# A token mixer with a product-key expert layer: tie slots filled on GpSimd, weight quarters summed on TensorE, half of the kept gaps made on VectorE

## The chip, the core and the metric

The kernel runs on one core of a Trainium2 chip. The metric is the device time of one execution in microseconds (us); smaller is better. Three runs of the kernel before gave 279.06, 279.29 and 279.59 us, median 279.29.

## The reference, cut to what matters

The input x has 8 rows of 512 tokens with 128 features. After a layer norm it goes through an attention layer of three branches (blocks, selected tokens, windows) and, beside it, through a product-key layer of experts; the output is x + attention * silu(experts). The change touches only the expert layer:

```python
q = (x @ Wq.T).reshape(b, n, 2, HEADS, DIM_KEY).transpose(2, 0, 1, 3, 4)
sim = jnp.einsum('pbnhd,hkpd->pbnhk', q, keys)          # 2 halves x 8 heads, 32 keys each
sx, ix = jax.lax.top_k(sim[0], TOPK)                    # TOPK = 16
sy, iy = jax.lax.top_k(sim[1], TOPK)
all_scores = (sx[..., :, None] + sy[..., None, :]).reshape(b, n, HEADS, TOPK * TOPK)
scores, pk_indices = jax.lax.top_k(all_scores, TOPK)
h = jax.nn.gelu(jnp.einsum('bnd,bnhkd->bnhk', x, W_down[pk_indices]), approximate=False)
h = h * jax.nn.softmax(scores, axis=-1)
return jnp.einsum('bnhk,bnhkd->bnd', h, W_up[pk_indices])
```

So each token needs, for each of 16 key vectors (2 halves, 8 heads), the 16 largest of 32 scores, in order; and then for each head the 16 largest of the sums of pairs. Of the 256 pairs of ranks only 50 can be among the 16 largest; the kernel calls them candidates. The expert of a pair hangs on the ranks alone, so one column per candidate is enough, and its weight is summed over the heads.

## The kernel before

**Tiles and blocks.** The 4096 tokens are 32 tiles of 128 tokens (one per partition). Four tiles make a block, a row of the input (8 blocks, b = 0 to 7). A first part loads, normalises and transposes everything and handles the first tiles; then `turn(n)` runs for n = 4 to 31 on every engine, with n = 4b + j. In this text "turn j" is the turn with that j. There is no scheduler: each engine has a `turn` of its own with its calls in an order written by hand, and the engines meet at semaphores alone. Each engine works strictly in its own order, so a wait holds up all that is queued behind it.

**One tile on its way.** Tile n is handled over five turns. TensorE's `scores(n)` (L1541) writes 16 x 32 scores into one of two PSUM banks, two turns ahead. VectorE takes the largest 8 of each vector (`first_8`, L1138), marks the scores that are at least the eighth (`mark_above`, L1151), strikes them out in a copy `rest` (`strike_above`, L1159), and takes the next 8 (`next_8`, L1191). With equal scores more than 8 can be marked; for that `rest` has 8 more columns per vector, the tie slots. `sum_above` (L1168) counts the marks, `spill_above` (L1177) makes 2 * count - rank of it, and `put_ties` (L1185) fills each slot with the eighth score where the count reaches that far and with a very small number elsewhere. Counts and the value between stand in the PSUM bank of the scores, which is free for the next scores only after `put_ties` (`sim_used`). Then TensorE transposes the 16 ranks (`top_columns`), forms the 50 pair sums of each head (`pair_gaps`), ScalarE copies them out (`take_gaps`), VectorE finds a bound (`gaps_of_pairs`, `gaps_of_thirds`, `last_gaps`).

One turn later GpSimd subtracts the bound (`past_of`, L480), ScalarE takes the sign (`side_of`), TensorE transposes it (`transpose_sides`, L1570), ScalarE copies it out (`take_sides`), GpSimd squares it (`square_of`, L496), and TensorE counts for each candidate how many beat it (`count_places`, L1582), the last call of its turn for j = 0, 1 and 2. In the turn after, ScalarE turns the count into a large number for a candidate that is out (`out_by_of`, L731), GpSimd adds the gap (`drop_of`, L502), and ScalarE takes eight exponentials with sums (`exps`, L826). In the fourth turn VectorE inverts the sums (`invert_sums`), and GpSimd multiplies (`weigh`, L510), adds heads 0-3 to heads 4-7 (`add_halves`, L517) and the two halves of that (`add_quarters`, L524). TensorE transposes the result, two heads wide, into the expert weights (`expert_weights`, L1596).

**The order around the change.** GpSimd, turn 0: `past_of(n-2)`, `drop_of(n-3)`, `weigh`, `add_halves`, `add_quarters(n-4)`, `square_of(n-2)`, from b = 2 on `gelu_times_weights`, then `scale_probs`. Turn 1 the same to `square_of`. Turn 2: from b = 2 on `gate_silu`, then `past_of`, `weigh`, `drop_of`, `add_halves`, `add_quarters`, `square_of`, `norm2`. Turn 3: `past_of`, from b = 2 on `gate_attention`, `weigh`, `drop_of`, `add_halves`, `square_of`, `add_quarters`, and from b = 2 on `add_input`. VectorE, every turn: `strike_above(n)`, half of `first_8(n+1)`, `sum_above(n)`, in turn 0 the attention's `maxima`, `invert_sums(n-4)`, `spill_above(n)`, the other half of `first_8`, `put_ties(n)`, `mark_above(n+1)`, `next_8` in two halves with `gaps_of_pairs(n-1)` between, `gaps_of_thirds`, `last_gaps`. TensorE's turn 1 ends with `expert_weights(n-4)`, `scores(n+2)`, `count_places(n-2)`, and its turn 2 begins with `attention_out` (L1726), after which ScalarE does `row_squares` (L852), `take_gaps` and `take_sides`.

## Time and profile before

| | |
|---|---|
| median of three runs | 279.29 us |
| the profiled execution: its own time | 281.1 us |
| the profiled execution: span of the profile | 279.4 us |
| mean granted TensorE clock | 0.982 |
| busy share of the span: VectorE (DVE) | 93% |
| GpSimd (POOL), ScalarE (ACT), TensorE (PE) | 81%, 84%, 85% |

The profile is of one execution. Its span is the time from the first to the last instruction on the core; the execution's own time is 1.7 us longer. L12 is line 12 of the kernel, a start is in us from the start of the span, and "idle before" is how long the engine had nothing to run, with the instruction that ended it. On one engine an instruction can start before the one before it has ended, so what an instruction costs its engine is the distance between starts and not its duration. Every block from the third on looks like every other: the same instruction stands 28.16 us further on.

### The profile page before, as it was taken

Reading aid. Unit: us, or ns where it says so; the run is one execution under the profiler, and the core shown is the slowest. Engines: PE = TensorE matmul, PEld = TensorE weight load, DVE = VectorE, ACT = ScalarE, POOL = GpSimd, SP = SyncE. Lnnn points to the kernel's source line nnn. Section 1 sums busy time; section 2 is a strip of 40 time slices with the busy share of each in tenths; the row PEclk is TensorE's granted clock in tenths of the full one; section 3 lists DMA queues with packets and bytes.
Section 4 is the critical chain, followed back from the end, with each engine's and each line's share of the span. In section 5 each row is a group of like instructions: output and inputs, shape, how many; then the busy total and the mean of one; then the engine's idle time right before and its main releaser. Section 6 shows DMA issues by size and latency. Waiting matters only on the chain.

```text
span 279.4 us, 7039 instructions
## 1 busy us (share of the span) xinstructions
PE 237.8 (85%) x1562; PEld 176.8 (63%) x1562; DVE 259.9 (93%) x1715; ACT 235.6 (84%) x1048; POOL 226.0 (81%) x344
## 2 busy tenths in 40 slices
PE   7899689797889888978898889888988898879891
PEld 7456243575577667766776577657765776568690
DVE  5899999969999999999999999999999999995885
ACT  2554766868989999899999999999999999996853
POOL 7889701447688899989898989898989898989672
PEclk9999999979999999999999999999999999997997
DMA  7920000000000000010001000100010001000102
GB/s 179 279 74 1 2 0 0 2 1 0 5 0 0 5 0 1 13 31 0 2 3 40 1 0 5 39 0 5 0 39 4 1 0 41 1 1 4 38 1 77
DMA packets 11228, 6.23 MB, mean 22 GB/s; under 512 B 1457, under 2 KB 10674, under 8 KB 11186
## 3 DMA queue, kind: packets, MB, share of 16 engines
q1 hardware_dynamic: 9858, 5.12, 6.9%
q10 hardware_dynamic: 1328, 0.66, 1.1%
q8 instruction: 13, 0.21, 0.3%
q14 instruction: 29, 0.24, 0.3%
HBM read 3.67 MB, written 2.10 MB: 21 GB/s over the span
## 4 chain that ended last, share of the span: by engine, by line
PE 32%; ACT 32%; POOL 19%; issue 13%; DVE 3%; POOLq 0%; ACTq 0%; DVEq 0%
ACT prob L837 6%; PE scratch L1640 4%; PE sim L1548 4%; ACT p_win L936 3%; POOL past L485 3%; POOL squareT L500 3%; ACT gap L759 3%; PE t_bank L1566 3%; ACT away L971 3%; PE s_bank L1742 3%; PE s_bank L1736 2%; ACT spare L856 2%; PE s_bank L1531 2%; ACT sideT L747 2%; ACT side L729 2%
## 5 line engine op out<-in xcount | busy, mean ns | idle before, releaser
L1194 DVE MAX8 top<-rest 128x8 f32<-128x40 f32 x512 | 57.2, 184 | 0.1
L1144 DVE MAX8 top<-sim 128x8 f32<-128x32 f32 x496 | 54.0, 181 | 2.0 <-PE sim L1548 1.9
L837 ACT ACTIVATE prob<-drop 128x50 f32<-128x50 f32 x224 | 51.5, 255 | 0.0
L837 ACT ACTIVATION_READ_ACCUMULATOR prob<-drop 128x1 f32 x224 | 47.1, 212 | 0.0
L500 POOL TENSOR_TENSOR squareT<-sideT 100x512 bf16<-100x512 bf16 x31 | 32.3, 1041 | 6.7 <-ACT sideT L747 6.6
L513 POOL TENSOR_TENSOR wgt<-prob,rden 128x400 f32<-128x400 f32 x30 | 25.7, 855 | 11.8 <-DVE rden L1136 11.7
L1548 PE MATMUL sim<-sim_w,xT_all 128*128 128x512 f32 x64 | 34.7, 625 | 0.5 <-ACT xT_all L784 0.5
L485 POOL TENSOR_TENSOR past<-gap,last 128x400 f32<-128x400 f32 x31 | 26.8, 863 | 9.8 <-DVE last L1218 9.8
L507 POOL TENSOR_TENSOR drop<-gap,out_by 128x400 f32<-128x400 f32 x30 | 31.0, 1033 | 1.1 <-ACT out_by L736 1.1
L1566 PE MATMUL t_bank<-gaps_of,topT 128*128 128x200 f32 x128 | 29.2, 352 | 1.7 <-ACT topT L752 1.7
L1218 DVE MAX8 last<-slot_gap 128x8 f32<-128x22 f32 x256 | 24.4, 168 | 1.1
L1566 PEld LDWEIGHTS t_bank<-gaps_of,topT 128*128 128x128 f32 x128 | 20.7, 191 | 4.4 <-ACT topT L752 2.6
L1592 PE MATMUL f_bank<-count_s,sideT 101*128 101x100 bf16 x124 | 15.1, 208 | 9.8 <-POOL squareT L500 9.8
L1592 PEld LDWEIGHTS f_bank<-count_s,sideT 101*128 101x128 bf16 x124 | 11.5, 98 | 18.4 <-issue 18.4
L1171 DVE TENSOR_REDUCE sim<-above 128x16 f32<-128x512 bf16 x32 | 21.7, 678 | 0.1
L1156 DVE TENSOR_TENSOR above<-sim,top 128x512 bf16<-128x512 f32 x32 | 21.7, 677 | 0.0
L1164 DVE SCALAR_TENSOR_TENSOR rest<-above,sim 128x512 f32<-128x512 bf16 x32 | 21.4, 669 | 0.2
L747 ACT ACTIVATE sideT<-f_bank 100x512 bf16<-100x512 f32 x31 | 18.8, 607 | 1.3 <-PE f_bank L1578 1.2
L759 ACT ACTIVATE gap<-t_bank 128x400 f32<-128x400 f32 x32 | 16.2, 505 | 3.9 <-PE t_bank L1566 2.6
L729 ACT ACTIVATE side<-past 128x400 bf16<-128x400 f32 x32 | 17.2, 536 | 2.0 <-POOL past L485 2.0
L521 POOL TENSOR_TENSOR wgt<-wgt 128x200 f32<-128x200 f32 x29 | 17.7, 609 | 1.1
L1647 PE MATMUL scratch<-xT_all,wc_sb 128*128 128x128 f32 x64 | 16.2, 409 | 0.0
(295 smaller groups left out, 753.1 us busy)
## 6 DMA issues: line engine op xcount, KB each, us to landing
out<-y_sb SPq DMA_DIRECT2D x7, 256.0 KB, 2.3
x_sb<-in_L_attn_hidden_states SPq DMA_DIRECT2D x2, 256.0 KB, 4.0
fwq_sb<-in_L_ffn_Wq ACTq DMA_DIRECT2D x2, 256.0 KB, 5.8
x_sb<-in_L_attn_hidden_states SPq DMA_DIRECT2D x1, 512.0 KB, 5.4
wc_sb<-in_L_attn_Wc SPq DMA_DIRECT2D x1, 256.0 KB
out<-last_y SPq DMA_DIRECT2D x2, 128.0 KB, 1.9
wo_in<-in_L_attn_Wo SPq DMA_DIRECT2D x1, 192.0 KB
keys_sb<-in_L_ffn_keys ACTq DMA_DIRECT2D x1, 128.0 KB, 3.4
```

The costliest lines, as they stand in the source:

```text
L485: nc.gpsimd.tensor_tensor(past[:, :, :], gap[n % 4][:, :, :], last8[n % 2][:, :, 7:8].to_broadcast([P, HEADS, CANDS]), ALU.subtract).then_ ...
L500: nc.gpsimd.tensor_tensor(squareT[0:TWO, :], sideT[0:TWO, :], sideT[0:TWO, :], ALU.mult).then_inc(square_done, 1)
L507: nc.gpsimd.tensor_tensor(drop[:, :, :], gap[n % 4][:, :, :], out_by[:, :, :], ALU.add).then_inc(drop_done, 1)
L513: nc.gpsimd.tensor_tensor(w[:, :, :], prob[n % 2][:, :, :], rden[n % 2][:, :].unsqueeze(2).to_broadcast([P, HEADS, CANDS]), ALU.mult).then ...
L759: nc.scalar.activation(gap[n % 4][:, :, :].rearrange("p h c -> p (h c)"), t_bank[:, 0:HEADS * CANDS], ACT.Copy).then_inc(gap_out, 1)
L837: last = nc.scalar.activation(prob[d][:, h, :], drop[:, h, :], ACT.Exp, scale=-1.0, accum_out=den[d][:, h:h + 1])
L1144: last = nc.vector.max(top[n % 3][:, v, 0:8], sim_bank[n % 2][:, bass.ts(v, KEYS)])
L1194: last = nc.vector.max(top[n % 3][:, v, 8:16], rest[:, v, :])
L1218: last = nc.vector.max(last8[n % 2][:, h, :], slot_gap[:, h, :])
L1548: mm(sim_bank[n % 2][:, :], xT_all[:, bass.ts(n, P)], sim_w[:, :], start=True, stop=True).then_inc(sim_ready, 1)
L1566: last = mm(t_bank[:, bass.ts(k, HALF_H * CANDS)], topT[:, bass.ts(k, P)], gaps_of[:, :, :].rearrange("p h c -> p (h c)"), start=True, sto ...
L1592: mm(o, one[0:TWO + 1, bass.ts(k, P)], count_s[0:TWO + 1, :], start=True, stop=False)
```

## The change

It does three things, and an order goes with each.

1. For the tiles of the turns (n = 4 to 31) the tie slots are filled by GpSimd: `ties_of(n)`, three instructions of 128 x 128 elements, stands right behind `past_of(n-2)` in GpSimd's turn (in turn 2 `gate_silu` goes behind both). The counts and the value between stand in SBUF (`counts`, `tie`, `tie_off`), since GpSimd works on SBUF here. VectorE's turn begins with `sum_above(n)`, ahead of `strike_above(n)`, and has neither `spill_above` nor `put_ties`; `next_8` waits for GpSimd (`ties_done`). The bank of the scores is free after `strike_above`. One small constant, `tie_rank`, is made by GpSimd at the start. Tiles 0 to 3 keep VectorE's two instructions.
2. `add_quarters` is gone: TensorE's `expert_weights` adds the quarters with two accumulating products in place of one transpose, and `wgt4` has two buffers instead of one.
3. For 14 tiles (3, 4, 7, 8, ... 27, 28; in turns 2 and 3) `out_by_of` on ScalarE and `drop_of` on GpSimd are replaced by one VectorE instruction, `keep_gaps`, which reads the counts from PSUM and takes the larger of the two values.

```diff
 rest = sb("rest", [P, VECS, KEYS + 8])
+counts = sb("counts", [P, VECS])
+tie_off = sb("tie_off", [P, VECS, 8])
+tie = sb("tie", [P, VECS, 8])
+tie_rank = sb("tie_rank", [P, 8])
 topT = sb("topT", [P, 2 * P])
...
 def summed(n):
     return n >= TILES - 4
+def kept_by_vector(n):
+    return TB - 1 <= n < TILES - 3 and n % TB in (0, TB - 1)
+def out_bys_until(n):
+    return sum(not kept_by_vector(m) for m in range(n + 1))
 def sums_until(n):
...
                         allow_small_or_imprecise_dtypes=True))
+    nc.gpsimd.tensor_scalar(tie_rank[:, :], rank_row[:, 7:15], 0.5, None, ALU.mult)
     def place(n_done, ins):
...
     def drop_of(n):
-        pool.wait_ge(out_by_done, n + 1)
+        if kept_by_vector(n):
+            return
+        pool.wait_ge(out_by_done, out_bys_until(n))
         if n >= 1:
...
     def add_halves(n):
         pool.wait_ge(wgt_done, n + 1)
-        w = wgt[n % 2]
-        nc.gpsimd.tensor_tensor(wgt4[:, :, :], w[:, 0:HEADS // 2, :], w[:, HEADS // 2:HEADS, :],
-                                ALU.add).then_inc(wgt4_done, 1)
-    def add_quarters(n):
-        pool.wait_ge(wgt4_done, n + 1)
         if n >= 2:
             pool.wait_ge(c_ready, n - 1)
-        nc.gpsimd.tensor_tensor(wgt2[n % 2][:, :, :], wgt4[:, 0:2, :], wgt4[:, 2:4, :],
-                                ALU.add).then_inc(wgt2_done, 1)
+        w = wgt[n % 2]
+        nc.gpsimd.tensor_tensor(wgt4[n % 2][:, :, :], w[:, 0:HEADS // 2, :], w[:, HEADS // 2:HEADS, :],
+                                ALU.add).then_inc(wgt4_done, 1)
+    def ties_of(n):
+        pool.wait_ge(summed_above, n + 1)
+        pool.wait_ge(top_done, 2 * n)
+        nc.gpsimd.tensor_tensor(tie[:, :, :], counts[:, :].unsqueeze(2).to_broadcast([P, VECS, 8]),
+                                tie_rank[:, :].unsqueeze(1).to_broadcast([P, VECS, 8]),
+                                ALU.subtract).then_inc(tie_step, 1)
+        pool.wait_ge(tie_step, 2 * (n - TB) + 1)
+        nc.gpsimd.tensor_scalar(tie_off[:, :, :], tie[:, :, :], SPILL, 0.0, ALU.mult, ALU.min
+                                ).then_inc(tie_step, 1)
+        pool.wait_ge(tie_step, 2 * (n - TB) + 2)
+        nc.gpsimd.tensor_tensor(rest[:, :, KEYS:KEYS + 8], tie_off[:, :, :],
+                                top[n % 3][:, :, 7:8].to_broadcast([P, VECS, 8]),
+                                ALU.add).then_inc(ties_done, 1)
     def gelu_times_weights(b):
...
         b, j = divmod(n, TB)
         if j == 0:
             past_of(n - 2)
+            ties_of(n)
             drop_of(n - 3)
             weigh(n - 4)
             add_halves(n - 4)
-            add_quarters(n - 4)
             square_of(n - 2)
             if b >= 2:
                 gelu_times_weights(b - 2)
             scale_probs(b - 1)
         elif j == 1:
             past_of(n - 2)
+            ties_of(n)
             drop_of(n - 3)
             weigh(n - 4)
             add_halves(n - 4)
-            add_quarters(n - 4)
             square_of(n - 2)
         elif j == 2:
+            past_of(n - 2)
+            ties_of(n)
             if b >= 2:
                 gate_silu(b - 2)
-            past_of(n - 2)
             weigh(n - 4)
             drop_of(n - 3)
             add_halves(n - 4)
-            add_quarters(n - 4)
             square_of(n - 2)
             norm2(b - 1)
         else:
             past_of(n - 2)
+            ties_of(n)
             if b >= 2:
                 gate_attention(b - 2)
             weigh(n - 4)
             drop_of(n - 3)
             add_halves(n - 4)
             square_of(n - 2)
-            add_quarters(n - 4)
             if b >= 2 and n < TILES - 1:
                 add_input(b - 2)
...
     def out_by_of(n):
+        if kept_by_vector(n):
+            return
         act.wait_ge(count_ready, n + 1)
...
             dve.wait_ge(summed_above, n)
+            dve.wait_ge(sim_used, n)
         nc.vector.tensor_tensor(above[:, :, :], sim_bank[n % 2][:, :].rearrange("p (v k) -> p v k", k=KEYS),
...
                                        sim_bank[n % 2][:, :].rearrange("p (v k) -> p v k", k=KEYS),
-                                       ALU.mult, ALU.add).then_inc(struck, 1)
+                                       ALU.mult, ALU.add).then_inc(sim_used, 1)
     def sum_above(n):
-        dve.wait_ge(struck, n + 1)
-        nc.vector.tensor_reduce(sim_bank[n % 2][:, 0:TIES], above[:, :, :], AX_X, ALU.add
-                                ).then_inc(summed_above, 1)
-    def tie_slots(n):
-        return sim_bank[n % 2][:, TIES:TIES + 8 * VECS].rearrange("p (v k) -> p v k", v=VECS)
+        dve.wait_ge(above_done, n + 1)
+        if n >= 1:
+            dve.wait_ge(ties_done, n)
+        nc.vector.tensor_reduce(counts[:, :], above[:, :, :], AX_X, ALU.add).then_inc(summed_above, 1)
     def spill_above(n):
         dve.wait_ge(summed_above, n + 1)
-        nc.vector.scalar_tensor_tensor(tie_slots(n),
-                                       sim_bank[n % 2][:, 0:TIES].unsqueeze(2).to_broadcast([P, VECS, 8]), 2.0,
+        nc.vector.scalar_tensor_tensor(tie[:, :, :], counts[:, :].unsqueeze(2).to_broadcast([P, VECS, 8]), 2.0,
                                        rank_row[:, 7:15].unsqueeze(1).to_broadcast([P, VECS, 8]),
...
     def put_ties(n):
         dve.wait_ge(spill_done, n + 1)
-        nc.vector.scalar_tensor_tensor(rest[:, :, KEYS:KEYS + 8], tie_slots(n), SPILL, eighth(n, 8),
-                                       ALU.mult, ALU.min).then_inc(sim_used, 1)
+        if n >= 1:
+            dve.wait_ge(top_done, 2 * n)
+        nc.vector.scalar_tensor_tensor(rest[:, :, KEYS:KEYS + 8], tie[:, :, :], SPILL, eighth(n, 8),
+                                       ALU.mult, ALU.min).then_inc(ties_done, 1)
     def next_8(n, h):
         dve.wait_ge(sim_used, n + 1)
+        dve.wait_ge(ties_done, n + 1)
         for v in range(h * HALF_V, (h + 1) * HALF_V):
...
                                 negate=True).then_inc(max_done, 1)
+    def keep_gaps(n):
+        dve.wait_ge(count_ready, n + 1)
+        dve.wait_ge(gap_out, n + 1)
+        dve.wait_ge(prob_done, n)
+        nc.vector.scalar_tensor_tensor(drop[:, :, :].rearrange("p h c -> p (h c)"),
+                                       f_bank[:, 0:HEADS * CANDS], OUT_SCALE,
+                                       gap[n % 4][:, :, :].rearrange("p h c -> p (h c)"),
+                                       ALU.mult, ALU.max).then_inc(drop_done, 1)
     def first_turns():
...
     def turn(n):
         b, j = divmod(n, TB)
+        sum_above(n)
         strike_above(n)
...
             first_8(n + 1, [0])
-        sum_above(n)
         if j == 0:
...
         invert_sums(n - 4)
-        spill_above(n)
+        if kept_by_vector(n - 3):
+            keep_gaps(n - 3)
         if n + 1 in tiles:
             first_8(n + 1, [1])
-        put_ties(n)
-        if n + 1 in tiles:
             mark_above(n + 1)
...
             pe.wait_ge(slot_gap_done, 2 * TILES)
+        elif n >= 1 and kept_by_vector(n - 1):
+            pe.wait_ge(drop_done, n)
         elif n >= 1:
-            pe.wait_ge(out_by_done, n)
+            pe.wait_ge(out_by_done, out_bys_until(n - 1))
         for k in range(HEADS // 2):
...
         o = dst[0:TWO, bass.ts(n % TB, P)]
-        if n < TILES - TB:
-            pe.wait_ge(wgt2_done, n + 1)
-            last = nc.tensor.transpose(o, wgt2[n % 2][:, :, :].rearrange("p h c -> p (h c)"), ident[:, :])
+        if n <= TILES - TB:
+            pe.wait_ge(wgt4_done, n + 1)
+            w, heads = wgt4[n % 2], HEADS // 2
+        elif n < TILES - 1:
+            pe.wait_ge(wgt_done, n + 1)
+            w, heads = (wgt if n < TILES - LAST else last_wgts)[n % 2], HEADS
         else:
-            if n == TILES - TB:
-                pe.wait_ge(wgt4_done, n + 1)
-                w, heads = wgt4, HEADS // 2
-            elif n < TILES - 1:
-                pe.wait_ge(wgt_done, n + 1)
-                w, heads = (wgt if n < TILES - LAST else last_wgts)[n % 2], HEADS
-            else:
-                pe.wait_ge(last_wgt, 1)
-                w, heads = last_wgts[n % 2], HEADS
-            for h in range(0, heads, 2):
-                last = mm(o, w[:, h:h + 2, :].rearrange("p h c -> p (h c)"),
-                          ident[:, :], start=(h == 0), stop=(h == heads - 2))
+            pe.wait_ge(last_wgt, 1)
+            w, heads = last_wgts[n % 2], HEADS
+        for h in range(0, heads, 2):
+            last = mm(o, w[:, h:h + 2, :].rearrange("p h c -> p (h c)"),
+                      ident[:, :], start=(h == 0), stop=(h == heads - 2))
         last.then_inc(c_ready, 1)
```

## Rows read from the trace of the kernel before

**Rows 1.** Busy time of each engine in one block of four turns, 193.16 to 221.32.
```profile
193.16:221.32 28.16, 24.61 (x171) 18.95 (x171) 27.47 (x197) 27.16 (x132) 26.31 (x36) 1.00 0.04 11
```

The columns of rows 1 are the stretch and its length, the busy us of PE, PEld, DVE, ACT and POOL, each with its number of instructions, the granted clock, the DMA share and GB/s.

**Rows 2.** The chain that ended last: start, us, the window exponentials of three blocks.
```profile
64.75 1.24 ACT p_win L936 x8
...
92.50 1.24 ACT p_win L936 x8
...
233.37 1.24 ACT p_win L936 x8
```

**Rows 3.** GpSimd's instructions in order of time in that block: start, us, what [idle before].
```profile
192.72 1.04 POOL L500 TENSOR_TENSOR squareT<-sideT 100x512 bf16<-100x512 bf16 x1 [0.24 <-ACT sideT L747]
...
197.86 1.04 POOL L507 TENSOR_TENSOR drop<-gap,out_by 128x400 f32<-128x400 f32 x1
...
199.43 1.03 POOL L500 TENSOR_TENSOR squareT<-sideT 100x512 bf16<-100x512 bf16 x1
...
202.02 0.85 POOL L485 TENSOR_TENSOR past<-gap,last 128x400 f32<-128x400 f32 x1
...
204.35 0.86 POOL L513 TENSOR_TENSOR wgt<-prob,rden 128x400 f32<-128x400 f32 x1 [0.49 <-DVE rden L1136]
205.28 0.61 POOL L521 TENSOR_TENSOR wgt<-wgt 128x200 f32<-128x200 f32 x1
205.97 0.40 POOL L528 TENSOR_TENSOR wgt<-wgt 128x100 f32<-128x100 f32 x1
206.32 1.04 POOL L500 TENSOR_TENSOR squareT<-sideT 100x512 bf16<-100x512 bf16 x1
...
210.27 0.86 POOL L485 TENSOR_TENSOR past<-gap,last 128x400 f32<-128x400 f32 x1
...
214.05 1.04 POOL L500 TENSOR_TENSOR squareT<-sideT 100x512 bf16<-100x512 bf16 x1
...
220.88 1.04 POOL L500 TENSOR_TENSOR squareT<-sideT 100x512 bf16<-100x512 bf16 x1 [0.24 <-ACT sideT L747]
```

**Rows 4.** TensorE in order of time: first product of two of the counts.
```profile
200.61 0.20 PE L1592 MATMUL f_bank<-count_s,sideT 101*128 101x100 bf16 x1 [0.34 <-POOL squareT L500]
...
215.30 0.21 PE L1592 MATMUL f_bank<-count_s,sideT 101*128 101x100 bf16 x1
```

**Rows 5.** ScalarE in order of time: the last step before the square.
```profile
220.18 0.62 ACT L747 ACTIVATE sideT<-f_bank 100x512 bf16<-100x512 f32 x1
```

**Rows 6.** Groups of instructions on GpSimd, by shape: mean ns after the comma.
```profile
L463 POOL TENSOR_SCALAR xn_all<-x_sb,rstd,nmr 128x128 f32<-128x128 f32 x16 | 7.0, 453 | 0.4
...
L573 POOL TENSOR_TENSOR p_cs<-p_cs,rgate 128x128 f32<-128x128 f32 x7 | 2.8, 400 | 0.0
L575 POOL TENSOR_TENSOR p_cs<-p_cs,rgate 64x64 f32<-64x64 f32 x7 | 2.0, 287 | 0.0
...
L408 POOL TENSOR_SCALAR off_mean<-ident 128x128 f32<-128x128 f32 x1 | 0.6, 552 | 0.0
```

**Rows 7.** VectorE in order of time, turn 1 of that block.
```profile
210.96 0.30 DVE L1180 SCALAR_TENSOR_TENSOR sim<-sim,rank_row 128x128 f32<-128x128 f32 x1
211.17 0.88 DVE L1144 MAX8 top<-sim 128x8 f32<-128x32 f32 x8
211.96 0.27 DVE L1188 SCALAR_TENSOR_TENSOR rest<-sim,top 128x128 f32<-128x128 f32 x1
212.15 0.68 DVE L1156 TENSOR_TENSOR above<-sim,top 128x512 bf16<-128x512 f32 x1
212.75 0.90 DVE L1194 MAX8 top<-rest 128x8 f32<-128x40 f32 x8
```

**Rows 8.** VectorE near the end: the kept gaps of the last two tiles.
```profile
266.01 0.56 DVE L1420 SCALAR_TENSOR_TENSOR last_drop<-f_bank,gap 128x400 f32<-128x400 f32 x1
266.49 0.55 DVE L1420 SCALAR_TENSOR_TENSOR last_drop<-t_bank,gap 128x400 f32<-128x400 f32 x1
```

**Rows 9.** GpSimd at the start of the span.
```profile
6.36 0.23 POOL L452 TENSOR_SCALAR var<-mv 128x4 f32<-128x4 f32 x1
```

More of the change, by code:

```diff
@@ L235, in program @@
         wgt = [sb(f"wgt{i}", [P, HEADS, CANDS]) for i in range(2)]
-        wgt4 = sb("wgt4", [P, HEADS // 2, CANDS])
-        wgt2 = [sb(f"wgt2_{i}", [P, 2, CANDS]) for i in range(2)]
+        wgt4 = [sb(f"wgt4_{i}", [P, HEADS // 2, CANDS]) for i in range(2)]
         last_drop = [sb(f"last_drop{i}", [P, HEADS, CANDS]) for i in range(2)]
@@ L274, in program @@
         sim_ready, sim_top8, sim_used, top_done = sem("sim_ready"), sem("sim_top8"), sem("sim_used"), sem("top_done")
-        above_done, struck, summed_above, spill_done = (
-            sem(n) for n in ("above_done", "struck", "summed_above", "spill_done"))
+        above_done, summed_above, spill_done, tie_step, ties_done = (
+            sem(n) for n in ("above_done", "summed_above", "spill_done", "tie_step", "ties_done"))
         topT_ready, topT_out, gap_ready, gap_out = (sem(n) for n in ("topT_ready", "topT_out", "gap_ready", "gap_out"))
@@ L286, in program @@
         half_out = sem("half_out")
-        wgt_done, wgt4_done, wgt2_done, c_ready, c_out = (
-            sem(n) for n in ("wgt_done", "wgt4_done", "wgt2_done", "c_ready", "c_out"))
+        wgt_done, wgt4_done, c_ready, c_out = (
+            sem(n) for n in ("wgt_done", "wgt4_done", "c_ready", "c_out"))
         last_past, last_square, last_kept, last_wgt, blocks_scaled = (
```

## The prediction

> **What bounds the kernel now.** I read the busy time of a block first, then the chain that ended last, then each engine in order of time. In a block of 28.16 us VectorE is busy 27.47, ScalarE 27.16, GpSimd 26.31, TensorE 24.61 [rows 1]. Three engines are within 7% of full, so no share of busy time says which one sets the period; an engine that is 97% busy may still be waiting in step with a loop through the others. The chain says so: between the window exponentials at 92.50 and at 233.37 [rows 2] there are five blocks of 28.17 each, and the chain in them runs through GpSimd, TensorE and ScalarE, hardly through VectorE. The interval before, 64.75 to 92.50, is 27.75: there GpSimd lacks the work that starts with b = 2.
>
> The loop of one block has three legs. They all stand in GpSimd's order of time [rows 3]:
> - **Leg A**, from `past` in turn 0 (202.02) to `squareT` in turn 1 (214.05): 12.03, GpSimd alone, with one wait of 0.49 for VectorE's reciprocal (at 204.35).
> - **Leg B**, from there to `squareT` in turn 2 (220.88): 6.83. GpSimd's own work is not what fills it. The square ends at 215.09, and TensorE starts to count at 215.30 [rows 4]. `count_places` is the last call of its turn 1, and `attention_out` is queued behind it, then ScalarE's row squares and copies of gaps and sides, the last from 220.18 for 0.62 [rows 5], and then the next square.
> - **Leg C**, from `squareT` in turn 2 (192.72) to `past` in turn 0 (202.02): 9.30, GpSimd alone without a wait.
>
> Sum 12.03 + 6.83 + 9.30 = 28.16. In leg B the handoff from a square to TensorE takes 0.15 where TensorE waits for it (the square of turn 3 runs from 199.43 for 1.03 [rows 3], TensorE follows at 200.61 [rows 4]), and here 0.21 pass. So TensorE's own queue has only some 0.06 us to spare: nearly all that delays the square of turn 1 delays the whole block.
>
> **The change, part by part.**
>
> *Tie slots on VectorE, removed.* The distance between starts is what counts: 210.96 to 211.17 and 211.96 to 212.15 [rows 7], 0.21 + 0.19 = 0.40 us in each of 28 turns.
>
> *Kept gaps on VectorE, added.* The nearest instruction is the same form at the end: 266.01 to 266.49, 0.48 us [rows 8], in two turns of four. VectorE's block gets 4 x 0.40 - 2 x 0.48 = 0.64 us lighter, 26.83 of work. The new order (count before strike) moves no work. Counts written to SBUF and not to PSUM: I cost it at nothing; one element is written for 32 read.
>
> *Tie slots on GpSimd, added.* Three instructions of 128 elements per partition. The first and third read two tensors: 0.40 us by the row of that very size [rows 6]. The second reads one: 0.45 by the two-operation form (453 ns), 0.55 by the one-operation form (552 ns) [rows 6]; I take 0.45, since it has two operations. Each of the second and third needs the one before: where an instruction waits for its forerunner the handoff is 0.08 (205.28 + 0.61 to 205.97 [rows 3]), where it doesn't, starts overlap ends by 0.04. So a tie fill holds GpSimd for 0.40 + 0.07 + 0.45 + 0.07 + 0.40 - 0.04 = 1.35 us. Bounds: 1.0 if each costs no more than the 64-element row (0.29) with the handoffs, 1.6 if the rows of 8 elements cost more than those of 50 and 80 that I see.
>
> Of the one-input instruction the rows say 453 ns, more than the 400 of two inputs. The Trainium skill (GPSIMD Engine Reference, 4.1 Engine selection) says that GpSimd is about half as fast as VectorE on two inputs but roughly at line rate on one. By that page the second instruction would take an estimated 0.3 us, a tie fill 1.2, and the time would be 284.1; the rows of this trace speak against it.
>
> *Quarters, removed.* A quarter starts at 205.97 and the square behind it at 206.32: 0.35, and the handoff before it goes too (205.28 to 205.97 becomes 0.57), so 0.47 in turns 0, 1 and 2, and 0.35 in turn 3, where the square stands between. TensorE gets two products in place of one transpose, one instruction more per turn: at the mean of rows 1, 24.61 / 171, some 0.14 us. I cost it at nothing, since TensorE has 3.5 us free per block; in turn 1 it stands ahead of the count, and that waits for the square anyway once the square is late. Without that cover it would add its 0.14 to leg B.
>
> *`drop` on GpSimd, removed in turns 2 and 3.* It lasts 1.04 us (197.86 [rows 3]), of which the next start overlaps 0.04: 1.00, less 0.10 because `add_halves` now follows directly on the `weigh` it needs: 0.90. ScalarE loses two `out_by`; neither stands between TensorE's count and the square in leg B, so I count no gain.
>
> *The constant at the start.* `tie_rank` stands between the last iota and the first variance, whose input VectorE has had ready (GpSimd ran into it without a wait at 6.36, 0.23 us [rows 9]). The chain goes through there: +0.2 us, once.
>
> **The loop after the change.**
> - Leg A: 12.03 - 0.49 (the reciprocal, which is no later, is now hidden behind the tie fill) + 2 x 1.35 - 2 x 0.47 = 13.30. No `drop` of turns 0 and 1 is taken away: those two stay on GpSimd.
> - Leg B: square 1.04, handoff 0.15, and from TensorE's count (215.30) to the next square (220.88) 5.58 as before: 6.77. GpSimd's own work between the squares (+1.35 for the tie fill, -0.90, -0.47) stays near 5.9 and waits at the end for the copy of the sides.
> - Leg C: 9.30 + 1.35 - 0.90 - 0.35 = 9.40.
>
> Sum 29.47, which is 1.31 more than 28.16. GpSimd's relief lies in the wrong turns: the two `drop`s go from turns 2 and 3, and the one in turn 2 is within leg B, where GpSimd has slack, while both tie fills of leg A lie on the loop.
>
> The new wait on VectorE: in turn 1 the `past` of GpSimd moves from 210.27 [rows 3] by -0.49 + 1.35 - 0.47 to 210.66, its tie fill ends near 212.9; VectorE would come to `next_8` at 212.75 - 0.40 = 212.35 [rows 7]. It waits 0.5 us, and half of `next_8`, the gaps and `last_gaps` are queued behind; but `past` of turn 2 isn't due before 216, so it costs nothing here. VectorE has 29.47 - 26.83 = 2.6 us per block for such waits.
>
> Over the run: five intervals, +6.6. From 233.37 on there is one leg A and B more, +1.2, after which the end hangs on other work that the change leaves alone. The interval from 64.75 to 92.50 has GpSimd idle and VectorE nearly full: -0.5, of its 0.64. Start +0.2. Together +7.5: a span of 279.4 + 7.5 = 286.9 and 288.6 for the profiled execution against its own 281.1. The profiled span is within 0.1 of the median of the runs, so the median goes from 279.29 to **286.8**. With tie fills between 1.15 and 1.6 the loop moves by 3 x -0.20 to 3 x 0.25 per block, some six blocks: 283.2 to 291.3.
>
> **The rivals.**
>
> *GpSimd alone is the bound (12%).* If leg B shrinks, say because ScalarE, freed of an `out_by`, delivers the sides sooner, the loop can't be shorter than GpSimd's own work. Busy 26.31 [rows 1] - 4 x 0.36 - 2 x 1.00 + 4 x 1.25 = 27.9, with handoffs about 28.7, 0.5 above 28.16: 279.3 + 6 x 0.5 - 0.3 = 282. For it: ScalarE is 27.16 busy now and gets lighter. Against: from 215.30 to the square at 220.88 the chain that ended last goes through TensorE and ScalarE with no wait for anything else, and the `out_by` isn't in it.
>
> *VectorE was the bound and is relieved (10%).* It is the busiest engine, 27.47 of 28.16. If the small instructions of the tie fill are so cheap on GpSimd that one holds it for less than about 0.91 us (1.35 - 1.31/3), the loop is no longer than before, and lighter VectorE and ScalarE let the block shrink by up to 0.64: 279.3 - 6 x 0.6 = 275.7. That point, 0.91, is where the sign turns. Against it: it is below three times the 287 ns of the 64-element row with the handoffs, 1.0.
>
> *VectorE waits for the ties and falls behind (7%).* If GpSimd reaches the tie fill in turns 0 to 2 a further us late, `next_8` slips by as much, the next `last_gaps` is late for `past`, and GpSimd and VectorE take turns waiting. One us more in two of four turns, partly hidden: 292 or more.
>
> **How the numbers follow.** The forecast, the loop through the square of turn 1, has 68% and by itself 283.2 to 291.3; GpSimd alone 12%; relieved VectorE 10%; late ties 7%; everything cancels 3%. The range reaches down to the second case and up to the forecast's own upper end: 281.5 to 291. A measurement of this kernel can tell about 0.2% from no change (0.6 us). Faster 0.10, same 0.03, slower 0.87.
>
> **What the profile after would show.** Right: window exponentials 29.5 us apart; the three tie instructions at 0.40, 0.45 and 0.40; TensorE idle before its count in turn 1, in place of none; GpSimd waiting near 0.9 us for the copy of the sides before the square of turn 2; VectorE's busy share down to about 88%, with a wait for GpSimd before the first `next_8` in turn 1. Wrong: a tie fill under 1.0 us; blocks of 28.7 or less with GpSimd never idle; or `past` waiting on `last_gaps`, which would mean that VectorE sets the pace.

## The result and the profile after

The change makes the kernel slower: median 295.04 us (four runs, 293.39 to 296.21) against 279.44 us of the kernel before beside it (279.06 to 279.95), ratio 1.0536 with a 95% interval of 1.0499 to 1.0572. The direction was forecast, the size was not: +7.5 forecast, +15.6 measured, and 295.04 lies outside the range of 281.5 to 291.

The profiled execution after took 294.93 us, its span is 293.2. From profile to profile that is +13.8; the profiled execution of before was itself 1.7 above its median, and the one of after is not. All that follows is counted from profile to profile. Some executions of a kernel show a lower granted clock and take over 1.5% longer than its fastest; the ratios and medians of the experiments below are of the others.

The page of the kernel after, its first and fourth part and one of its groups:

```profile
span 293.2 us, 7306 instructions
PE 247.7 (84%) x1646; PEld 186.6 (64%) x1646; DVE 258.0 (88%) x1673; ACT 232.0 (79%) x1034; POOL 241.3 (82%) x387
POOL 49%; PE 24%; issue 13%; ACT 11%; DVE 2%; POOLq 0%; DVEq 0%; ACTq 0%
...
L548 POOL TENSOR_SCALAR tie_off<-tie 128x128 f32<-128x128 f32 x28 | 17.9, 639 | 2.4
```

VectorE went from 93% to 88% busy, as forecast, and is only 2% of the chain that ended last; GpSimd is half of it, where it was 19% before. One block, 199.97 to 230.45, in the columns of rows 1:

```profile
199.97:230.45 30.48, 26.14 (x185) 20.40 (x184) 27.24 (x192) 26.73 (x129) 28.45 (x42) 1.00 0.04 10
```

It is 30.48 us long instead of 28.16 [rows 1], and GpSimd is now the busiest engine. Its instructions in order of time, that block, against [rows 3]:

```profile
199.97 1.04 POOL L512 TENSOR_TENSOR squareT<-sideT 100x512 bf16<-100x512 bf16 x1 [0.86 <-ACT sideT L773]
...
209.65 0.87 POOL L497 TENSOR_TENSOR past<-gap,last 128x400 f32<-128x400 f32 x1
...
218.50 0.85 POOL L497 TENSOR_TENSOR past<-gap,last 128x400 f32<-128x400 f32 x1
219.32 0.40 POOL L544 TENSOR_TENSOR tie<-counts,tie_rank 128x128 f32<-128x128 f32 x1
219.81 0.64 POOL L548 TENSOR_SCALAR tie_off<-tie 128x128 f32<-128x128 f32 x1
220.53 0.42 POOL L551 TENSOR_TENSOR rest<-tie_off,top 128x128 f32<-128x128 f32 x1
220.91 1.03 POOL L521 TENSOR_TENSOR drop<-gap,out_by 128x400 f32<-128x400 f32 x1
...
222.83 0.61 POOL L537 TENSOR_TENSOR wgt<-wgt 128x200 f32<-128x200 f32 x1
223.40 1.03 POOL L512 TENSOR_TENSOR squareT<-sideT 100x512 bf16<-100x512 bf16 x1
...
230.45 1.04 POOL L512 TENSOR_TENSOR squareT<-sideT 100x512 bf16<-100x512 bf16 x1 [0.86 <-ACT sideT L773]
```

The legs read off these starts:

| leg | before | forecast | after |
|---|---|---|---|
| A, `past` turn 0 to `squareT` turn 1 | 12.03 | 13.30 | 13.75 |
| B, to `squareT` turn 2 | 6.83 | 6.77 | 7.05 |
| C, to `past` turn 0 | 9.30 | 9.40 | 9.68 |
| block | 28.16 | 29.47 | 30.48 |

TensorE in order of time, turn 1 of that block, against [rows 4]:

```profile
223.49 0.68 PE L1654 MATMUL c_bank<-ident,wgt 128*100 128x128 f32 x4 [0.90 <-POOL wgt L537]
224.01 1.02 PE L1584 MATMUL sim<-sim_w,xT_all 128*128 128x512 f32 x2
224.87 0.21 PE L1630 MATMUL f_bank<-count_s,sideT 101*128 101x100 bf16 x1
```

And the same stretch in the chain that ended last:

```profile
222.83 0.62 POOL wgt L537
223.45 0.04 issue
223.49 0.68 PE c_bank L1654 x4
224.17 0.86 PE sim L1584 x2
```

Here is something that the forecast did not have: the chain leaves GpSimd before the square. TensorE waits 0.90 for the halves, does the products (four passes for two fp32 products) and the scores, and only then counts, 1.47 after the square's start. The square alone would have let it count after 1.04 + 0.15.

The kernel before has to be read again here, in leg A, which the forecast took for GpSimd's alone. The chain that ended last leaves GpSimd there: from `past` in turn 0 it goes over ScalarE and then through TensorE's own queue into the count:

```profile
208.23 1.12 ACT prob L837 x9
...
214.60 0.86 PE sim L1548 x2
```

The count follows the scores at 215.30 without a wait, while the square would have allowed it at 215.09 + 0.15 = 215.24. So it is the square, with GpSimd's leg A before it, that had 0.06 to spare, and TensorE's queue had nothing. The two ways were almost equally long; the tie fills lengthened that of GpSimd, and it took over.

**Where the 13.8 us are**, by the first window exponential of a block in each trace: up to the first -1.47 (63.17 against 64.64; forecast +0.2); the next interval +0.72 (28.47 against 27.75; forecast -0.5); the five intervals after it +11.15 (152.03 against 140.88; forecast +6.6); from there to the end +3.4 (49.5 against 46.1; forecast +1.2).

Part of the ends is TensorE's clock. Before, it was granted 0.61 between 58 and 62, and 1.00 after. The chain runs through TensorE there in both; the scores, before and after:

```profile
59.20 1.71 PE sim L1548 x2
...
58.73 0.86 PE sim L1584 x2
```

That is 0.85, and the three projections around them took 0.75, 0.64 and 0.49 on the chain before and 0.39, 0.33 and 0.33 after: 1.68 together. Without the clock the start would have been 0.21 later, not 1.47 earlier, and the count ahead of these instructions does start 0.21 later (57.48 against 57.27). After, the clock falls near the end, and the products and scores of the last leg B take 1.18 and 1.71 on the chain, where the block above has 0.68 and 0.86: 1.35 of the end's loss. The window of the kernel after, in the columns of rows 1:

```profile
252.00:256.00 4.00, 3.08 (x10) 1.76 (x9) 3.53 (x25) 4.00 (x23) 3.92 (x6) 0.72 0.01 2
```

TensorE's instructions in it, in order of time:

```profile
253.96 1.18 PE L1654 MATMUL c_bank<-ident,wgt 128*100 128x128 f32 x4 [0.90 <-POOL wgt L537]
254.93 1.92 PE L1584 MATMUL sim<-sim_w,xT_all 128*128 128x512 f32 x2
```

### The profile page after: what moved, and what is told of

The parts are those of the page before. It is cut to its first block, busy times and chain, and to the rows that moved or that the text cites. A ratio compares the mean times of both kernels' runs of the same rounds, so it can differ in the third digit from the quotient of the medians.

```text
span 293.2 us, 7306 instructions
## 1 busy us (share of the span) xinstructions
PE 247.7 (84%) x1646; PEld 186.6 (64%) x1646; DVE 258.0 (88%) x1673; ACT 232.0 (79%) x1034; POOL 241.3 (82%) x387
## 4 chain that ended last, share of the span: by engine, by line
POOL 49%; PE 24%; issue 13%; ACT 11%; DVE 2%; POOLq 0%; DVEq 0%; ACTq 0%
POOL squareT L512 8%; POOL wgt L527 6%; POOL past L497 5%; POOL tie_off L548 4%; PE sim L1584 4%; POOL drop L521 3%; PE s_bank L1776 3%; POOL y L622 3%; POOL actT L560 3%; POOL tie L544 2%; PE s_bank L1770 2%; ACT spare L882 2%; PE s_bank L1567 2%; ACT sideT L773 2%; PE c_bank L1654 2%
## 5 line engine op out<-in xcount | busy, mean ns | idle before, releaser
L1654 PE MATMUL c_bank<-ident,wgt 128*100 128x128 f32 x112 | 18.5, 289 | 12.3 <-POOL wgt L537 12.3
L1654 PEld LDWEIGHTS c_bank<-ident,wgt 128*100 128x100 f32 x112 | 14.2, 170 | 19.5 <-issue 10.5
L778 ACT ACTIVATE topT<-t_bank 128x256 f32<-128x256 f32 x32 | 12.5, 390 | 12.7 <-PE t_bank L1593 12.7
L1200 DVE TENSOR_REDUCE counts<-above 128x16 f32<-128x512 bf16 x32 | 21.5, 670 | 0.0
L548 POOL TENSOR_SCALAR tie_off<-tie 128x128 f32<-128x128 f32 x28 | 17.9, 639 | 2.4
```

Of the source, the lines that this page charges most:

```text
L548: nc.gpsimd.tensor_scalar(tie_off[:, :, :], tie[:, :, :], SPILL, 0.0, ALU.mult, ALU.min).then_inc(tie_step, 1)
L1654: last = mm(o, w[:, h:h + 2, :].rearrange("p h c -> p (h c)"), ident[:, :], start=(h == 0), stop=(h == heads - 2))
```

## The experiments

Theory 1: the block is the loop through the square of turn 1, as forecast; the tie fill is longer than costed, and in turn 1 the products stand on the loop. Theory 2: VectorE's wait for the ties (0.43 in turn 1) hands its delay on and sets the block. "Block" below is the distance between two steady first `maxima` of the attention in turn 0 (28.16 before, 30.48 after). Times of before are those of the same chip.

**Products later.** The change, with TensorE's products of turn 1 moved behind the count:

```diff
     project_window(b, U_KW, wk_sb)
-    expert_weights(n - 4)
...
     pair_gaps(n - 1)
+    expert_weights(n - 5)
     project_window(b, U_VW, wv_sb)
```

> The changed kernel with one call moved on TensorE: the expert weights of turn 1 go behind attention_out and pair_gaps of turn 2, so that the count of turn 1 follows the scores directly. Theory 1 (the block is the loop of GpSimd from the square of turn 2 round to the square of turn 1, and TensorE and ScalarE from there to the next square): the count starts 0.15 us after the square instead of some 0.45, the block goes from 30.48 to about 30.2, the time from 295.0 to about 293.2. GpSimd's own work is 29.6 per block, so it can't fall below that. Theory 2 (VectorE's waits for the tie slots set the block): no change, 295.

Measured: 293.20 against 280.29 us, ratio 1.0440 (1.0396 to 1.0484), block 30.22. The count waits for the square again (e1, TensorE in turn 1; the square starts at 223.71):

```profile
222.74 1.02 PE L1584 MATMUL sim<-sim_w,xT_all 128*128 128x512 f32 x2
224.89 0.20 PE L1630 MATMUL f_bank<-count_s,sideT 101*128 101x100 bf16 x1 [1.13 <-POOL squareT L512]
```

1.18 from the square's start to the count in place of 1.47: the products' place costs 0.26 of the 2.32 per block, as theory 1 has it.

**The square ahead of the weights too.** As before, and in GpSimd's turn 1 `square_of` before `weigh` and `add_halves`:

```diff
     drop_of(n - 3)
+    square_of(n - 2)
     weigh(n - 4)
     add_halves(n - 4)
-    square_of(n - 2)
```

> The changed kernel with the expert weights of turn 1 behind the attention of turn 2, as in the first run, and the square of turn 1 ahead of weigh and add_halves on GpSimd. Theory 1: leg A loses 1.5 us and the loop is no longer the longest; what is left is GpSimd's own work of 29.6 us per block, hence a block of 29.6 to 29.8 and 290 to 291 us. If the loop was not the cause: 293 as in the first run.

Measured: 287.61 against 280.23 us, ratio 1.0282 (1.0238 to 1.0326), block 29.57, just under what was expected; the time is 2.4 us under its range of 290 to 291. Against e1, 1.75 of the 5.6 us lie ahead of the first `maxima`, where TensorE was granted 0.50 to 0.71 between 58 and 62 there and 1.00 here. GpSimd in order of time, one block apart:

```profile
176.08 0.87 POOL L497 TENSOR_TENSOR past<-gap,last 128x400 f32<-128x400 f32 x1
...
205.63 0.87 POOL L497 TENSOR_TENSOR past<-gap,last 128x400 f32<-128x400 f32 x1
```

In all 42 instructions of that block the view names no wait for another engine. So 29.55 is GpSimd's own work with the changed division, in this order: another could at most hide some of the handoffs between dependent instructions. The loop stood 0.9 above it, and even this block is 1.4 above the 28.16 of the kernel before. Had VectorE's waits set the block, moving `weigh` behind the square could not have helped.

**Parts of the change undone.** The kept gaps (`kept_by_vector` returns False), the quarters (`add_quarters` and one transpose again), the ties (back on VectorE, but with their values in SBUF as in the changed kernel):

```diff
 def kept_by_vector(n):
-    return TB - 1 <= n < TILES - 3 and n % TB in (0, TB - 1)
+    return False
```

> The changed kernel with no kept gaps on VectorE: all tiles go by ScalarE's out_by and GpSimd's drop again. Theory 1: leg C gets 0.9 us longer, in leg B the drop fits into GpSimd's wait of 0.86, block about 31.4, time about 300.5. Theory 2 (VectorE, with its waits for the ties, sets the block): VectorE is relieved of 0.96 per block, the time stays or falls, 289 to 295.

Measured: 302.40 against 280.29 us, ratio 1.0793 (1.0747 to 1.0840), 1.9 above what was expected. Its five steady blocks are 31.02, 32.87, 31.36, 31.36 and 32.91; the 31.36 is read below, and why two are longer is open. The `drop` of turn 3 comes back into leg C with its 0.90; that of turn 2 falls into leg B's slack. This is the price that theory 1 gives. GpSimd's own work gives the same, 29.55 + 2 x 0.90 = 31.35; theory 2 is out by either.

```diff
     add_halves(n - 4)
+    add_quarters(n - 4)
...
-    if n <= TILES - TB:
+    if n < TILES - TB:
+        pe.wait_ge(wgt2_done, n + 1)
+        nc.tensor.transpose(o, wgt2[n % 2][:, :, :].rearrange("p h c -> p (h c)"),
+                            ident[:, :]).then_inc(c_ready, 1)
+        return
```

> The changed kernel with the quarters back on GpSimd and one transpose on TensorE. Theory 1: leg A gets 2 x 0.47 longer, leg C 0.35, leg B 0.2 to 0.3 shorter (TensorE has 0.6 less ahead of the count), block about 31.5, time about 301. Theory 2 (the products on TensorE are the cost): faster than the changed kernel, below 292.

Measured: 304.26 against 280.29 us, ratio 1.0845 (1.0789 to 1.0901), 3 above what was expected. The trace is of an execution of 308.61, at a mean granted clock of 0.948. Its five steady blocks are 35.20, 31.52, 33.07, 31.51 and 31.52. Three are the 31.5 of theory 1, 1.0 above the change; how much of the two long ones stands in the 304.26, no trace shows.

```diff
     past_of(n - 2)
-    ties_of(n)
...
     invert_sums(n - 4)
+    spill_above(n)
     first_8(n + 1, [1])
+    put_ties(n)
     mark_above(n + 1)
```

> The changed kernel with the tie slots back on VectorE in all turns (its two instructions, on SBUF), GpSimd's three gone. Theory 1: legs A and C lose 2 and 1 tie fills of 1.6 us, the loop falls under VectorE's own work, which is then 26.8 + 1.6 = 28.4 per block; block 28.5 to 28.7, time 283 to 285, still over the kernel before because of the kept gaps on VectorE. Theory 2 (the two products per tile on TensorE are what costs): it stays over 290.

Measured: 306.47 against 280.29 us, ratio 1.0890 (1.0808 to 1.0972), block 32.5 on average. This missed theory 1 by more than 20 us. It is over 290, as the rival with the products had it, but far above the changed kernel, which the products can't explain: they are the same in both. The groups of VectorE in e2, by shape:

```profile
L1201 DVE SCALAR_TENSOR_TENSOR tie<-counts,rank_row 128x128 f32<-128x128 f32 x32 | 24.1, 753 | 0.1
L1210 DVE SCALAR_TENSOR_TENSOR rest<-tie,top 128x128 f32<-128x128 f32 x32 | 19.9, 621 | 0.2
```

Before, the same two instructions take 292 and 274 ns on average:

```profile
L1180 DVE SCALAR_TENSOR_TENSOR sim<-sim,rank_row 128x128 f32<-128x128 f32 x32 | 9.3, 292 | 0.1
...
L1188 DVE SCALAR_TENSOR_TENSOR rest<-sim,top 128x128 f32<-128x128 f32 x32 | 8.8, 274 | 0.2
```

The difference is where counts and tie values stand: in the PSUM bank before, so that only one input of each comes from SBUF; here both do. That gave theory 3: VectorE, with both inputs in SBUF, waits for GpSimd.

**SBUF or PSUM, alone.** The kernel before, with counts and tie values in SBUF and nothing moved:

```diff
-    nc.vector.tensor_reduce(sim_bank[n % 2][:, 0:TIES], above[:, :, :], AX_X, ALU.add
+    nc.vector.tensor_reduce(counts[:, :], above[:, :, :], AX_X, ALU.add
...
-        return sim_bank[n % 2][:, TIES:TIES + 8 * VECS].rearrange("p (v k) -> p v k", v=VECS)
+        return tie[:, :, :]
```

> The kernel before with nothing moved between engines: only the counts and the value between stand in SBUF and not in the PSUM bank of the scores. Theory 3 (from the run with the ties back on VectorE, where these two instructions took 753 and 621 ns in the mean and up to 2.3 us, ending where GpSimd's instruction beside them ended: a VectorE instruction with both inputs in SBUF waits until GpSimd is between instructions): both grow by 0.3 us or more in the mean, 0.7 a turn, and the time goes to 297 to 305. Rival (that run was slow for its order of calls): both stay at 292 and 274 ns and the time at 279 to 281.

Measured: 299.47 against 280.23 us, ratio 1.0691 (1.0655 to 1.0727), block 31.2. Two operands moved from PSUM to SBUF cost 19 us. One of them in VectorE's order of time in c1:

```profile
161.76 2.22 DVE L1182 SCALAR_TENSOR_TENSOR tie<-counts,rank_row 128x128 f32<-128x128 f32 x1
```

and GpSimd beside it:

```profile
161.18 0.86 POOL L487 TENSOR_TENSOR past<-gap,last 128x400 f32<-128x400 f32 x1
162.00 1.03 POOL L509 TENSOR_TENSOR drop<-gap,out_by 128x400 f32<-128x400 f32 x1
162.98 0.85 POOL L515 TENSOR_TENSOR wgt<-prob,rden 128x400 f32<-128x400 f32 x1
163.91 0.60 POOL L523 TENSOR_TENSOR wgt<-wgt 128x200 f32<-128x200 f32 x1
```

`past`, `drop` and `weigh` follow each other without a gap to 163.83, and the next one needs the one before and starts at 163.91. In just that gap VectorE's instruction gets through, after 2.22 us, and ends at 163.98. It is no single case: of the 64 instances of the two instructions in c1 30 took more than 0.4 us, and 27 of these ended 0.07 to 0.20 after a start on GpSimd. GpSimd's durations hardly change (`add_halves` 0.63 on the mean against 0.61). The Trainium skill (GPSIMD Engine Reference, 1. Specifications) says that the two engines share their SBUF interfaces and lists a VectorE instruction with two SBUF inputs as a case of contention; the trace agrees and its numbers are 0.39 and 0.40 us more on the mean, 1.9 in this instance.

So e2 doesn't tell what the tie fill on GpSimd costs. That needs the ties as they were, in PSUM.

**The change less its tie fill.** The kernel before with kept gaps in both turns and the products; ties untouched:

```diff
     invert_sums(n - 4)
+    if kept_by_vector(n - 3):
+        keep_gaps(n - 3)
     spill_above(n)
...
     add_halves(n - 4)
-    add_quarters(n - 4)
```

> The kernel before with the kept gaps on VectorE and the products on TensorE, as in the changed kernel, but with the tie slots on VectorE and in PSUM as before: the changed kernel less its tie fill. Theory 1: the loop is shorter than before (28.16 - 0.90 - 0.35 and some 0.6 more on TensorE ahead of the count: about 27.5), so VectorE's work of 27.5 + 0.96 = 28.4 sets the block, 28.5 to 28.8, time 282 to 284. Against the 295 of the changed kernel that makes the tie fill some 12 us of its loss. If instead the products are the cost, it is 290 or more.

Measured: 282.70 against 280.23 us, ratio 1.0104 (1.0051 to 1.0156), block 28.58. So, with the other two parts in place, the tie fill makes 1.90 of the 2.32 us per block, and 1.0536 / 1.0104 = 1.043 of the ratio. The tie fill alone on the kernel before was not run. Its first `maxima`, one block apart, in VectorE's order of time:

```profile
175.97 0.49 DVE L1273 TENSOR_REDUCE nmax<-s_bank 128x4 f32<-128x320 f32 x1 [0.33 <-PE s_bank L1696]
...
204.55 0.49 DVE L1273 TENSOR_REDUCE nmax<-s_bank 128x4 f32<-128x320 f32 x1 [0.33 <-PE s_bank L1696]
```

A stretch of 30 us in the columns of rows 1 (VectorE 29.50 busy, GpSimd 24.35). The chain of a block runs on VectorE from the `maxima` to the kept gap of turn 3, and from there through TensorE back to the `maxima`:

```profile
180.00:210.00 30.00, 27.15 (x196) 21.38 (x197) 29.50 (x214) 27.96 (x143) 24.35 (x33) 1.00 0.04 10
```

**The other parts alone, on the kernel before.** Kept gaps in both turns; kept gaps in turn 3 only (n % 4 == 0); the latter with turn 3's quarters by products; products in all turns:

```diff
+    return TB - 1 <= n < TILES - 3 and n % TB in (0, TB - 1)
...
+    return TB - 1 <= n < TILES - 3 and n % TB == 0
...
 def add_quarters(n):
+    if n % TB == TB - 1:
+        return
...
-    add_quarters(n - 4)
```

> The kernel before with the kept gaps of two turns in four on VectorE and nothing else. Theory 1: VectorE's work of 28.4 per block sets it, block 28.5 to 28.7, time 282 to 284, the same as with the products added.

> The kernel before with one kept gap per block on VectorE, that of turn 3 (tiles 4, 8, ... 28), and nothing else of the change. Theory 1: leg C loses 0.9 us on GpSimd and the loop falls to 27.3; VectorE's work is 27.5 + 0.48 = 27.95 and sets the block at 28.0 to 28.2; time 278.5 to 280.5, at best 0.5% under the kernel before.

> The run before, and in turn 3 also the quarters by two products on TensorE. Leg C is another 0.35 shorter but no longer the bound; the products, four passes and 0.6 us more, stand on TensorE ahead of the window scores that VectorE's maxima wait for. Theory 1: no gain over it, 279 to 281.

> The kernel before with the quarters of all turns by products on TensorE and nothing else. Theory 1: leg C is 0.35 shorter; on TensorE 0.57 more stands ahead of the count of turn 1, which sets leg A and B together; block 28.3 to 28.5, time 280.5 to 282.

| kernel | us (before 280.21) | ratio (95%) | block |
|---|---|---|---|
| kept gaps, both turns | 281.02 | 1.0035 (1.0011 to 1.0058) | 28.32 |
| kept gaps, turn 3 | 280.32 | 1.0014 (0.9987 to 1.0042) | 28.06 |
| the same with its products | 281.61 | 1.0073 (1.0047 to 1.0100) | 28.33 |
| products, all turns | 282.98 | 1.0106 (1.0070 to 1.0141) | 28.58 |

Kept gaps in both turns came out below what was expected: VectorE's 27.47 and 2 x 0.44 make 28.35, and the block is 28.32, so VectorE has no other waits left. The products were dearer than expected: 282.98 where 280.5 to 282 was, and the version of turn 3 with its products 0.6 above its 279 to 281. TensorE in turn 1 of that kernel:

```profile
186.36 0.60 PE L1606 MATMUL c_bank<-ident,wgt 128*100 128x128 f32 x4
186.79 1.02 PE L1538 MATMUL sim<-sim_w,xT_all 128*128 128x512 f32 x2
187.66 0.21 PE L1582 MATMUL f_bank<-count_s,sideT 101*128 101x100 bf16 x1
```

The products take 0.43 from start to start; the transpose in the trace before takes 0.11 (214.33 to 214.44). That is 0.32 of the 0.42 per block, in a queue that had nothing to spare. The remaining 0.1 lies in turn 3: there the chain of this kernel no longer goes over GpSimd's next `past`, as before, but from the square through TensorE, with that turn's products on it:

```profile
201.65 0.48 PE c_bank L1606 x4
```

From the square of turn 2 to the copy of the gaps ahead of the exponentials it takes 12.08 this way (193.23 to 205.31), where GpSimd's way took 11.97 (192.72 to 204.69). So GpSimd's savings of 0.47 and 0.35 buy nothing here. Kept gaps in turn 3 alone are the only part that shortens the block, by 0.10, and in the time that can't be told from no change. No version that was run beats the kernel before.

**What an instruction of 128 elements costs on GpSimd.** The changed kernel with twelve more instructions on GpSimd, ahead of its first `past`:

```diff
+    nc.gpsimd.tensor_scalar(m[0][:, :, :], m_in[:, :, :], 1e30, 0.0, ALU.mult, ALU.min)
...
+    nc.gpsimd.tensor_scalar(flat(m[2]), flat(m_in), 1e30, 0.0, ALU.mult, ALU.add)
+    nc.gpsimd.tensor_scalar(flat(m[3]), flat(m_in), rstd1[:, 0:1], nmr1[:, 0:1], ALU.mult, ALU.add)
+    nc.gpsimd.tensor_scalar(flat(m[4]), flat(m_in), rstd1[:, 0:1], nmr1[:, 0:1], ALU.mult, ALU.min)
+    nc.gpsimd.tensor_scalar(flat(m[5]), flat(m_in), 1e30, None, ALU.mult)
+    nc.gpsimd.tensor_scalar(flat(m[6]), flat(m_in), 0.0, None, ALU.min)
+    nc.gpsimd.tensor_tensor(flat(m[7]), flat(m_in), flat(m_in), ALU.add)
...
```

> The changed kernel with 12 more GpSimd instructions of 128 elements where GpSimd is idle, ahead of the first past; each writes a tile of its own. a: mult, min by constants on 16 x 8; b: the same flat; c: mult, add by constants; d: mult, add by columns; e: mult, min by columns; f: mult alone; g: min alone; h: two inputs, add; i: two inputs, mult; j: second input repeated 8 times; k: output strided; l: one input a single repeated value. If the form with constants costs more than that with columns: c 550 to 640, d 453. If min costs more than add: e above d, b above c. If the 16 x 8 shape costs: a above b. The changed kernel has 639 for a, 425 for the last instruction of the tie fill, 402 for the first.

GpSimd in order of time in that kernel (`ma` is m[0], the form of the tie fill, `mb` the same with a flat shape, `mc` to `mh` are m[2] to m[7]):

```profile
34.49 0.64 POOL L684 TENSOR_SCALAR ma_out<-m_in 128x128 f32<-128x128 f32 x1
35.20 0.64 POOL L685 TENSOR_SCALAR mb_out<-m_in 128x128 f32<-128x128 f32 x1
35.90 0.30 POOL L686 TENSOR_SCALAR mc_out<-m_in 128x128 f32<-128x128 f32 x1
36.28 0.45 POOL L687 TENSOR_SCALAR md_out<-m_in,rstd,nmr 128x128 f32<-128x128 f32 x1
36.72 0.79 POOL L688 TENSOR_SCALAR me_out<-m_in,rstd,nmr 128x128 f32<-128x128 f32 x1
37.57 0.53 POOL L689 TENSOR_SCALAR mf_out<-m_in 128x128 f32<-128x128 f32 x1
38.17 0.53 POOL L690 TENSOR_SCALAR mg_out<-m_in 128x128 f32<-128x128 f32 x1
38.67 0.40 POOL L691 TENSOR_TENSOR mh_out<-m_in 128x128 f32<-128x128 f32 x1
```

The shape doesn't matter, the pair of operations does: multiply and add by constants 0.30, by columns 0.45; multiply and minimum by constants 0.64, by columns 0.79. The minimum costs 0.34 more in either. One operation alone, 0.53, costs more than multiply and add. The four forms with two inputs that are not shown took 0.40 to 0.42. This is one execution with one instance of each; it took 299.47 us, since the added work holds back the first `past` by 6.8.

## Why the prediction was right and wrong

**The structure was right.** After the change the block is the loop of three legs; the reliefs lie in the wrong turns; VectorE, 88% busy, doesn't set it. VectorE waited 0.43 for the ties in turn 1 (forecast 0.5) and it cost nothing, as e6 shows, where no instruction of GpSimd waits for VectorE:

```profile
221.05 0.91 DVE L1221 MAX8 top<-rest 128x8 f32<-128x40 f32 x8 [0.43 <-POOL rest L551]
```

GpSimd waited 0.86 before the square of turn 2 (forecast 0.9). The first and third tie instruction took 0.40 and 0.42 (forecast 0.40 each). One sign did not come: TensorE was to be idle before its count in turn 1, and it was busy with the scores, as the products had held them back.

**First step that failed: "I take 0.45, since it has two operations".** The second tie instruction takes 0.64. The row chosen [rows 6] is multiply and add; the change has multiply and minimum, and e5 shows that this pair is another price. A tie fill holds GpSimd for 219.32 to 220.91 = 1.59 and not 1.35. Three of them are on the loop: +0.72 per block, in leg A 0.48 (13.30 to 13.78; measured 13.75), in leg C 0.24 (9.40 to 9.64; measured 9.68). Over five blocks and one more leg A that is 4.1 of the 6.3 us by which the forecast fell short. The value was within the bounds of 1.0 to 1.6; "nearest row" was the nearest in size and in number of operations, not in kind. The Trainium skill's rule (GPSIMD Engine Reference, 4.1 Engine selection: one input near line rate), put at 0.3 us in the prediction, fits only multiply and add by constants, 0.30; for the form in the change it is off by a factor of two.

**Second step that failed: "I cost it at nothing ... that waits for the square anyway".** Two errors stand in it. The price came from the mean of all TensorE instructions, 0.14; these are fp32 products that run as four passes, 0.68 us with the chain on them. And the cover was looked for in the wrong place: the products wait for `add_halves`, which ends with the square's start, so they run beside the square and, with the scores behind them, last longer than it: the count starts 2.04 after the halves (222.83 to 224.87), and would start 0.57 + 1.04 + 0.15 = 1.76 after them behind the square alone. Leg B is 7.05 and not 6.77: +0.28, and e1, without them there, gets 0.26 back; over five blocks and one more leg B 1.7 us. The prediction's reading that TensorE's own queue had 0.06 to spare exchanges the two ways into the count: the square had that, the queue nothing. With both terms at their measured size the sum is 13.78 + 7.05 + 9.64 = 30.47; measured 30.48.

**The ends.** Five intervals at +1.31 were 6.6; at +2.32 they would be 11.6, and 11.15 came, the first of them being 30.12. The tail was given one leg A and B: at measured sizes 1.72 + 0.22 = 1.94, and 1.35 more came from the lower granted clock, together 3.3 of 3.4.

**Third step that failed: "VectorE nearly full: -0.5".** The interval that was to gain 0.5 lost 0.72. VectorE got lighter (27.04 busy of 28.47, before 27.58 of 27.75), but it was not on the chain of that interval before either: that ran through ScalarE and TensorE, `exps` alone 19% of it. So a lighter VectorE had nothing to give there. After, the chain takes in the products of turn 1 and the tie fills of turns 3 and 0:

```profile
72.56 0.44 PE c_bank L1654 x4
...
88.98 0.64 POOL tie_off L548
```

The start was right: `tie_rank` takes 0.24 at 6.35, the next instruction starts 0.29 later (6.65 against 6.36), and 0.21 are left at the count of 57.48, for the +0.2 of the forecast. The lower clock of the profiled execution of before covers it, 1.68.

**The base.** The sum was made against the profiled execution, 288.6 against the 294.93 measured: 6.3 short. The terms make that up: tie fill 4.1, products 1.7, the interval that gained nothing 1.2, the clock near the end 1.35, less 1.7 for the clock of before near 60 and 0.4 for the first of the five intervals. The two levels of the clock nearly cancel, which is luck. Put onto the median it became 286.8, 8.2 short, since the profiled execution of before, 281.1, had 1.8 us that the median of 279.29 lacks, and that of after doesn't have them. "The profiled span is within 0.1 of the median" hid this: it sets a span, which leaves out the 1.7 that lie around it, against times that have them. The 1.68 of the clock near 60 is of that size; that it is what the other executions lack is likely, but not shown.

**The rivals.** GpSimd alone (28.7 per block) was not the bound of the changed kernel, and e6 gives its real height, 29.55: its own sum with a tie fill of 1.59 is 28.7 + 4 x 0.24 = 29.7. VectorE relieved needed a tie fill under 0.91; it was 1.59. Late ties gave 292 or more, near the result, but not by that way: the loop and not VectorE's wait made the time.

## What to carry to other kernels

- Price a new instruction by a row with the same pair of operations, not only the same engine and size; where there is none, the bound is worth as much attention as the sum: the upper one, 1.6, was right here. Here a saving of 0.40 us on VectorE became 1.59 us on GpSimd.
- A product that replaces a transpose is not "one instruction more": count its passes, and look at what it waits for and what is queued behind it. An engine with 3.5 us free per block had nothing free at the place that counts.
- Two ways can lead into one event and end within 0.06 of each other, as the square and TensorE's queue did before the count. Price a change against both.
- Reliefs pay only on the loop that sets the time. The kept gaps cost 0.16 per block in the balanced kernel, the products 0.42, both together 0.42; once the tie fill has put GpSimd on the loop they give 0.9 and 1.0 back.

## What was not expected of the hardware

- A VectorE instruction with both inputs in SBUF waits, when GpSimd is at work, until it is between two instructions: 292 and 274 ns became 678 and 676 on the mean, once 2.22 us, and the kernel 19 us slower for two small operands moved out of PSUM. The order of the changed kernel escapes it by giving both instructions to GpSimd.
- On GpSimd, 128 elements per partition cost from 0.30 to 0.79 us by the operations and by whether the numbers are constants or columns, and one operation costs more than multiply and add. Why was not settled, and a tie fill without the minimum was not tried.
